# Rebuilding the opening of a cross-attention and mixture-of-experts kernel: load order, weight split and first projections

## The reference

```
x = x + xattn(layernorm(x), ctx)        # 32 batches, 128 tokens, width 128, 16 heads of 64
    # q = xn @ Wq, k = ctx @ Wk, v = ctx @ Wv (W_qkv is 128 x 3072); softmax(q k / 8) v; @ W_out + b_out
x = x + moe(layernorm(x))               # 16 experts, the best 2 of each token, softmax of their two logits
    # gate/up = t @ Wgu[e] + bgu[e]; (clip(up) + 1) * gate * sigmoid(1.702 gate); @ Wd[e] + bd[e]
```

## Time and profile before

| | us |
|---|---|
| median of three runs | 624.29 (623.92 to 624.73) |
| profiled execution, its own time | 624.85 |
| its span, first to last instruction | 623.1 |
| TensorE busy (share of span) | 536.6 (86%) |
| VectorE busy | 535.1 (86%) |
| ScalarE busy | 490.9 (79%) |
| GpSimd busy | 446.2 (72%) |
| DMA at the opening (4 to 12 us) | 300 to 374 GB/s |

### The profile page before, as it was taken

How to read it: one execution, slowest core, us unless ns; L and a number is a source line. 1 busy time by engine, 2 the same in 40 slices (tenths; PEclk the granted TensorE clock), 3 DMA queues, 4 the chain that set the end, 5 groups by cost and what they waited for, 6 DMA issues and landing times.

```text
span 623.1 us, 20538 instructions
## 1 busy us (share of the span) xinstructions
PE 536.6 (86%) x6805; PEld 454.5 (73%) x6806; DVE 535.1 (86%) x1526; ACT 490.9 (79%) x1423; POOL 446.2 (72%) x555
## 2 busy tenths in 40 slices
PE   0689999999999999999999999999756989898700
PEld 0357989888898998988889989998642766666500
DVE  5789999999999999999999999999965877677515
ACT  0479999999999999999999999999832666666500
POOL 7174766689898898988989889877264377777720
PEclk9989999999999999999999999999976999999955
DMA  9689131228316285622932741576012343332149
GB/s 259 188 306 326 28 71 28 43 62 306 84 33 191 60 307 163 228 55 55 312 82 36 251 142 38 145 254 130 3 33 52 91 111 95 94 86 81 41 130 274
DMA packets 76820, 82.14 MB, mean 132 GB/s; under 512 B 8324, under 2 KB 56476, under 8 KB 76724
## 3 DMA queue, kind: packets, MB, share of 16 engines
q1 hardware_dynamic: 63124, 68.13, 38.3%
q0 software_dynamic: 4608, 8.47, 4.2%
q10 hardware_dynamic: 8992, 4.30, 2.6%
HBM read 19.35 MB, written 46.84 MB: 106 GB/s over the span
## 4 chain that ended last, share of the span: by engine, by line
PE 72%; DVE 8%; issue 5%; DMA 5%; ACT 4%; POOL 2%; SPq 2%; ACTq 1%; POOLq 0%; DVEq 0%
PE bank L1156 17%; PE bank L1157 16%; PE bank L1158 16%; PE bank L1252 8%; PE bank L1302 5%; PE bank L1327 3%; PE bank L1335 2%; DMA ctx_sb<-results 2%; DMA ctx_sb<-in_ctx_dram 2%; PE bank L1384 2%; PE bank L1362 1%; PE bank L1166 1%; PE bank L1282 1%; ACT probs L525 1%; POOL places L698 1%
## 5 line engine op out<-in xcount | busy, mean ns | idle before, releaser
L525 ACT ACTIVATE probs<-bank,nbias 128x128 f32<-128x128 f32 x512 | 146.4, 369 | 4.2
L755 POOL DMA_INDIRECT results<-z,stage x80 | 80.3, 1004 | 41.4 <-ACT z L570 23.5
L1000 DVE TENSOR_TENSOR pT<-bank,pT 128x512 f16<-128x512 f32 x128 | 87.2, 682 | 6.5 <-ACT pT L537 5.2
L979 DVE TENSOR_REDUCE qmax<-bank 128x4 f32<-128x512 f32 x128 | 87.0, 679 | 0.0
L1156 PE MATMUL bank<-keys,q_pad 128*128 128x128 f16 x480 | 86.6, 219 | 0.0
L1158 PE MATMUL bank<-keys,q_pad 128*128 128x128 f16 x480 | 86.6, 219 | 0.0
L1157 PE MATMUL bank<-keys,q_pad 128*128 128x128 f16 x480 | 86.6, 219 | 0.0
L537 ACT ACTIVATE pT<-bank 128x512 f16<-128x512 f32 x128 | 78.3, 612 | 4.1 <-PE bank L1252 4.0
L1252 PE MATMUL bank<-ident,probs 128*128 128x128 f32 x512 | 79.2, 278 | 2.2 <-DVE pT L1000 2.1
L698 POOL DMA_INDIRECT places<-payload,slots x64 | 65.4, 1022 | 16.4 <-issue 12.2
L1156 PE MATMUL bank<-xT,w_qkv 128*128 128x256 f16 x256 | 71.7, 280 | 2.6 <-DVE xT L819 1.7
(11 more groups left out here) (220 smaller groups left out, 2007.3 us busy)
## 6 DMA issues: line engine op xcount, KB each, us to landing
places<-z SPq DMA_DIRECT2D x8, 4160.0 KB, 14.7
q_pad<-q_nat SPq DMA_DIRECT2D x120, 128.0 KB, 2.4
stage<-places SPq DMA_DIRECT2D x80, 65.0 KB, 1.9
ctx_sb<-results SPq DMA_DIRECT2D x16, 256.0 KB, 5.7
ctx_sb<-in_ctx_dram ACTq DMA_DIRECT2D x4, 512.0 KB, 10.4
stage<-in_L_ffn_Wgu_dram SPq DMA_DIRECT2D x1, 2048.0 KB, 8.8
out_dram<-x_sb ACTq DMA_DIRECT2D x8, 256.0 KB, 5.4
stage<-in_L_xattn_W_qkv_dram SPq DMA_DIRECT2D x3, 512.0 KB, 6.3
```

What stands on the lines that cost most here:

```text
L525: last = nc.scalar.activation(probs[:, b, k, :], score_bank[b][:, k * P:(k + 1) * P], ACT.Exp, bias=nbias[:, b, k:k + 1], scale=exp_scale)
L755: nc.gpsimd.indirect_dma_start(out=results, out_offset=bass.IndirectOffsetOnAxis(ap=to, axis=0), in_=z[:, (u - 5) % NZ, t, :], in_offset=None,
L979: nc.vector.tensor_reduce(qmax[:, r % 2, :], score_bank[r % 2][:, :].rearrange("p (h k) -> p h k", h=4), AX.X, ALU.max).then_inc(s["qmax_o ...
L1000: nc.vector.tensor_tensor(pT[:, r % 2, LO, :], pt_bank[:, :], pT[:, r % 2, HI, :], ALU.subtract).then_inc(s["pt_lo"], 1)
```

## The change

- SP loads x's four batches ahead of the W thirds. ScalarE's queue issues the five small arrays ahead of ctx. ScalarE runs a tiny activation before its first wait.
- The factor of W is made by itself (`first_spread`, `first_scale`), as soon as the three W thirds are in, with the magnitude of ctx part 0 between its two halves. The factor of ctx follows after part 3.
- ScalarE writes `hi` of thirds 0 and 1 and also scales them in place in fp32; GpSimd scales third 2 in place, and ScalarE then writes its `hi`. GpSimd writes all three `lo` as a plain difference. DVE does none of this.
- GpSimd normalises the rows of pairs 0 and 1 (DVE did).
- ScalarE scales ctx for pair 0 after the W thirds, not before.
- The factors `fac` are made ahead of the first items, from PSUM.
- Four banks, not two, take the first q and k items, so item t waits for the low half of item t - 4. Scores of pair 0 wait for all eight items.
- TensorE runs 13 matmuls of 512 zero columns (`warm`) between and before the first products.

```diff
-        first_bank = (qk_bank, pt_bank)
+        first_bank = (qk_bank, pt_bank, score_bank[0], score_bank[1])
@@ SyncE
+            sp.dma_start(x_sb[:, 0:4, :], x[0:4]...).then_inc(in_x[0], 16)
             for c in range(3): ... W_qkv thirds
-            sp.dma_start(x_sb[:, 0:4, :], x[0:4]...).then_inc(in_x[0], 16)
@@ ScalarE
-            for c in range(4): ... ctx
             ... bout_bc, bg_bc, wg_nat, bgu_sb, bd_sb
+            for c in range(4): ... ctx
+            act.wait_ge(s["zeroed"], 6)
+            nc.scalar.activation(spare[:, :], zeros[:, 0:1], ACT.Copy)
             act.wait_ge(s["scales"], 1)
-            scale_ctx(0)
-            for c in range(3):
+            for c in range(2):
                 nc.scalar.activation(w_qkv[:, HI, third], stage[:, third], ACT.Copy, scale=scale_to[:, 0:1]) -> w_hi
-                if c == 0:
-                    ... xT high half; scale_ctx(1)
+                act.wait_ge(s["w_hi"], c + 1)
+                nc.scalar.activation(stage[:, third], stage[:, third], ACT.Copy, scale=scale_to[:, 0:1]) -> w_scaled
+            act.wait_ge(s["v_scaled"], 1)
+            nc.scalar.activation(w_qkv[:, HI, 2 * INNER:3 * INNER], stage[:, 2 * INNER:3 * INNER], ACT.Copy) -> w_hi
+            act.wait_ge(s["scales"], 2)
+            scale_ctx(0)
+            ... xT high half; scale_ctx(1)
@@ GpSimd
             inverse_root("stat_agg", 2, mv, var_eps, rstd, "rstd_ok", 1)
+            normal_rows(0)
+            pool.wait_ge(s["scales"], 1)
+            nc.gpsimd.tensor_scalar(stage[v third], stage[v third], scale_to[:, 0:1], None, ALU.mult) -> v_scaled
+            for c in range(3):
+                pool.wait_ge(s["w_hi"], c + 1)
+                if c < 2:
+                    pool.wait_ge(s["w_scaled"], c + 1)
+                nc.gpsimd.tensor_tensor(w_qkv[:, LO, third], stage[:, third], w_qkv[:, HI, third], ALU.subtract) -> w_lo
             inverse_root("stat_agg", 4, mv, var_eps, rstd, "rstd_ok", 2)
+            normal_rows(1)
@@ VectorE
+            dve.wait_ge(in_x[0], 16)
+            prep_stats(0)
             for c in range(3): ... W magnitudes
-            ... statistics, ctx magnitudes, both factors, prep_rows(0)
+            magnitude(0, part_largest[:, 0:3])
+            largest_row(score_bank[0])
+            ctx_magnitude(0)
+            first_scale(score_bank[0], 0)
+            for c in range(1, 4):
+                ctx_magnitude(c)
+            magnitude(1, part_largest[:, 3:7])
+            largest_row(score_bank[1])
+            first_scale(score_bank[1], 1)
+            make_factors(score_bank[1])
+            prep_stats(1)
-            qkv_low(0) ... qkv_low(1) ... qkv_low(2), prep_stats(1), prep_rows(1), fac between the items
+            prep_low(0, 0)
+            for t in range(4):
+                first_low(t)
@@ TensorE
-            spread(score_bank[0], 0, 2)
+            def warm(n):
+                for k in range(n):
+                    nc.tensor.matmul(o_bank[:, :], ident16[:, :], zeros[:, :].bitcast(F16)[:, 0:512], start=True, stop=True)
+            def first_spread(bank, k):
+                pe.wait_ge(s["absmax"], k + 1)
+                nc.tensor.transpose(bank[0:1, 0:P], largest[:, k:k + 1], ident[:, :]) -> largest_mm
+                pe.wait_ge(s["row_max_ok"], spreads[0])
+                nc.tensor.matmul(bank[:, P:P + 1], ones2[0:1, :], row_max[0:1, 0:1], start=True, stop=True) -> spread_mm
+            first_spread(score_bank[0], 0)
             pe.wait_ge(s["in_small"], 16 * 5)
             ... transpose of Wg
+            pe.wait_ge(in_ctx[2], 16)
+            warm(7)
+            first_spread(score_bank[1], 1)
+            warm(3)
             prep(0)
+            warm(3)
             for t in range(8):
-                project_qk(0, 0, t, first_bank[t % 2])
+                project_qk(0, 0, t, first_bank[t % 4])
-                    wait(pe, "first_split", t - 1)
+                    wait(pe, "first_split", t - 3)
-                                wait(pe, "first_split", 4 + 2 * r)
+                                wait(pe, "first_split", 8)
```

More of the change, by code:

```diff
@@ L439, in _ @@
             act.dma_start(bd_sb[:, :], bd.rearrange("e (k f) -> (e k) f", k=8)).then_inc(s["in_small"], 16)
+            for c in range(4):
+                act.dma_start(ctx_sb[:, 8 * c:8 * c + 8, :], ctx[8 * c:8 * c + 8].rearrange("b t d -> t b d")).then_inc(in_ctx[c], 16)
+            act.wait_ge(s["zeroed"], 6)
+            nc.scalar.activation(spare[:, :], zeros[:, 0:1], ACT.Copy)
             def scale_ctx(q):
@@ L495, in weights_high @@
                 if (p, r) == (0, 2):
-                    act.wait_ge(s["scales"], 2)
+                    act.wait_ge(s["scales"], 3)
                     nc.scalar.activation(w_out[:, HI].rearrange("p b n -> p (b n)"), stage[:, 3 * INNER:4096], ACT.Copy,
@@ L825, in v_low, with largest_row, first_scale, ctx_magnitude @@
                                         v[:, par, HI, k // 2, heads, 0:DH], ALU.subtract).then_inc(s["misc_free"], 1)
+            def largest_row(bank):
+                spreads[0] += 1
+                dve.wait_ge(s["largest_mm"], spreads[0])
+                nc.vector.tensor_reduce(row_max[0:1, :], bank[0:1, 0:P], AX.X, ALU.max).then_inc(s["row_max_ok"], 1)
+            def first_scale(bank, k):
+                dve.wait_ge(s["spread_mm"], spreads[0])
+                at_top = bank[:, P + 1:P + 2]
+                link(nc.vector.tensor_scalar(at_top, bank[:, P:P + 1], TINY, 1.0 / TOP, ALU.max, ALU.mult))
+                link(nc.vector.tensor_copy(scale_from[:, k:k + 1], at_top))
+                nc.vector.reciprocal(scale_to[:, k:k + 1], at_top).then_inc(s["scales"], 1)
+            def ctx_magnitude(c):
+                dve.wait_ge(in_ctx[c], 16)
+                part_magnitude(ctx_sb[:, 8 * c:8 * c + 8, :].rearrange("p b d -> p (b d)"))
+            def make_factors(bank):
+                both, three_of = bank[:, P + 2:P + 3], bank[:, P + 3:P + 4]
+                link(nc.vector.tensor_tensor(both, bank[:, P + 1:P + 2], scale_from[:, 0:1], ALU.mult))
+                link(nc.vector.tensor_copy(fac[:, 1:2], both))
+                link(nc.vector.tensor_tensor(three_of, both, scale_from[:, 0:1], ALU.mult))
+                link(nc.vector.tensor_copy(fac[:, 4:5], three_of))
+                link(nc.vector.tensor_scalar(fac[:, 0:1], three_of, DH ** -0.5, None, ALU.mult))
+                nc.vector.tensor_scalar(fac[:, 2:3], three_of, -DH ** -0.5, None, ALU.mult).then_inc(s["factors"], 1)
+            dve.wait_ge(in_x[0], 16)
+            prep_stats(0)
             for c in range(3):
@@ L829, in _ @@
                 part_magnitude(stage[:, c * INNER:(c + 1) * INNER])
[L830 to L834, removed]
+            dve.wait_ge(s["part_max"], 3)
+            magnitude(0, part_largest[:, 0:3])
+            dve.wait_ge(s["consts"], 7)
+            largest_row(score_bank[0])
+            ctx_magnitude(0)
@@ L913, in weight_scales @@
                     make_scales(2, 3, "scales")
-                    dve.wait_ge(s["scales"], 2)
+                    dve.wait_ge(s["scales"], 3)
                     link(nc.vector.tensor_tensor(fac[:, 3:4], fac[:, 1:2], scale_from[:, 2:3], ALU.mult))
```

54 lines of the change are left out of this document (17 added, 37 removed).

## The result

After the change the kernel takes 629.08 us (median of 6 runs, 627.61 to 629.89); the kernel before takes 624.76 beside it (6 runs, 623.92 to 626.0). The ratio is 1.0071 (95%: 1.0055 to 1.0087): slower by 4.3 us, where 4.5 off was forecast. The profiled execution took 629.89, the slowest of the six, with a span of 628.0.

The account below looks back on a forecast made before the run. TensorE and DVE were taken as busy throughout the steady part, so the opening adds to the time in full. 4.8 us gained there less 0.3 set aside gave 4.5 off: 619.8 us, range 618.2 to 622.8.

Parts of the forecast that it names:

- After it: After the items: x's other batches land about 31.2, needed at 33.5; clock fall at 42 stays; 0.3 us set aside.
- rival 2: Pair 0: x's rest lands near 35, sharing DMA with Wd and first clear; DVE waits about 1.5; 621.4 us; chance 0.09.
- Its last sentence: Sign of a wrong prediction: shift at 33 us not found at 80, a wait in pair 0 replacing the old one.
- Loads: Opening DMA: last W third lands at 9.3 us (9.1 before), last ctx part at 15.6, 0 to 0.8 late.
- Factor of W: Opening: W's scale factor, made by itself, is out at 13.4 us, 5.9 us earlier.
- ScalarE and GpSimd on W: Opening: GpSimd scales the v third in 3.5 us, differences take 2.2; low halves ready at 19.7, 21.9 and 24.1.
- rival 4: Opening: GpSimd becomes the bound if its four large ops cost about twice as much; slower, 629.8 us; chance 0.09.
- Rivals 1: First items: TensorE's clock rises only near 28.5 us; gain 2.3, time 622.0; chance 0.12.
- The items: Pair 0's projections: first item at 22.5 us, clock up between 21.6 and 25, 13 DVE ops of 0.62 taking 8.1.
- yardstick: End of DVE's last v item in the opening: 32.7 us, 4.8 ahead of 37.48.

Follow-up runs that it names:

- with ctx first: Kernel after with ctx issued ahead of the five small arrays again: 625.65 us, ratio 1.0023 to the kernel before.
- late clear: Kernel after with the second clear issued behind pair 2's q moves: 620.57 us, ratio 0.9936; the same in the kernel before: 624.62 us, 1.0004.
- two ablations: Kernel after with the late clear, without the 13 warm matmuls: ratio 0.9979; with two banks in place of four for the first items: 0.9974.
- all repairs at once: Kernel after with the late clear, small arrays behind ctx, and the transpose of wg_nat behind the first items: 620.67 us, ratio 0.9950.
- versions with ctx's factor 2 us earlier: Late clear, small arrays behind ctx, wg_nat's transpose late: ratio 0.9950; also x behind W: 0.9921; also six warm matmuls behind the second spread: 0.9922.

## Why the prediction was wrong

*The step that failed* is the one headed "After it". It followed x's other batches and the fall of the clock at 42 us and stopped there. It should have gone on along SP's queue. The prediction had x's other batches land 0.6 later (31.2 against 30.6) and saw, in rival 2, that Wd and the first clear would be issued earlier; it asked of them only whether they delay x. The second clear waits for the first to land, on DMA engines that are full from 24 us on in the kernel before (share 1.06), so an earlier issue does not bring it forward: with ctx first, where x's rest is issued as in the kernel before, it is 0.2 later than before. The prediction had the pair steps 4.8 earlier. It let the two run against each other without a look at where they meet. They meet at pair 1's moves, where before has 0.6 us of slack.

An estimate of the wait is the lead of the scores, plus the delay of the clear, less the slack of 0.6. It gives 2.2 + 3.0 - 0.6 = 4.6 for the kernel after (5.4 measured) and 3.7 + 0.2 - 0.6 = 3.3 with ctx first (2.9 measured). By the prediction's own lead of 4.8 it gives 4.4 to 4.8. So the forecast gain could not have passed there, however good the opening. Its last sentence named this symptom, a wait in pair 0 that takes the place of the old one, but gave it no price. The late clear shows that this is the decisive step: without the wait the kernel is 4.05 us faster, and the same move gives the old kernel nothing. That 4.05 lies so near the forecast 4.5 is luck: at the first scores the lead was 3.1, not 4.8. What the wait cost: 5.4 us, and 1.1 more by 71 us, where TensorE's clock was at 1.2 GHz after standing; some of it is caught up by the tables (4.7 to 4.2).

*Loads* were mis-sized, as a term. Forecast: last W third 9.3, last ctx part 15.6 "0 to 0.8 late for the small packets". Measured: 11.38 and 18.29. By the runs that put them back, x ahead of W costs W about 1.2 to 1.45, the small arrays cost ctx 2.55 to 3.0. The five issues took 3.8 us, not 2.3, so ctx's first issue comes at 4.61 instead of 0.79. The mistake was to let ctx land almost on time all the same. In 2 to 6 us few bytes flow in the kernel after, and they are not caught up: the windows 2 to 4 and 4 to 6 us show 77 and 136 GB/s, before it was 257 and 354. That is 0.8 MB less, an estimated 2.1 us at the 380 GB/s around 7 us.

```profile
4.61 8.54 ACTq L439 DMA_DIRECT2D ctx_sb<-in_ctx_dram  x4
```

```profile
2.00:4.00 2.00, 0.00 (x0) 0.00 (x0) 0.00 (x0) 0.00 (x0) 1.86 (x10) 1.00 0.52 77
```

DVE had ctx's maximum at 19.7, not 17.3. From there on the serial path was as forecast: 19.7 to 24.97 is 5.3, against 17.3 to 22.5, 5.2.

*Factor of W*: out at 15.3 against 13.4, late by the load and nothing else (11.38 to 15.3 is 3.9; 9.3 to 13.4 is 4.1).

*ScalarE and GpSimd on W*: right. The v third took 2.85 (3.5 taken, bounds 0.22 and 4.9) and stayed under the 4.1 from which it costs; the differences took 2.1 each (2.2), the last ended at 24.5 (24.1), and no item waited for it. By the Trainium skill's line-rate (GPSIMD Engine Reference, § 4.1 Engine selection) the v third is an estimated 0.9 us, worked out from the same page of the Trainium skill (1.03 cycles an element in § 3.1, 1.2 GHz in § 1 Specifications), and not the prediction's 1.1; the measured 2.85 is three times that, and the measurement decides. The warning of contention in the same page of the Trainium skill (§ 8 Key points), which stood in rival 4, was hardly put to the test: each difference took 2.1, but beside them DVE ran reductions of one input and tiny operations. GpSimd never became the bound; the slower side came true by another mechanism, which no rival named. Rivals 1 and 2 did not come either: the clock was up at 25.8, and x's other batches landed at 33.6, 2.5 us before DVE took them at 36.1.

*The items*: right, as a length. From the first projection to the end of the last v item, 24.97 to 35.12 is 10.15 us; the forecast was 22.5 to 32.7, 10.2; before took 14.6. The clock was up at 25.8, DVE started an op every 0.60 to 0.65. The two ablations give part of it to the warm matmuls (0.8 to 1.3) and the banks (1.4 to 2.0). What the work taken off DVE gave was not measured alone.

*The sum at the last v item*, the prediction's yardstick: 4.8 forecast, 2.4 measured (37.48 to 35.12); the missing 2.4 are the loads, by which DVE had ctx's maximum 2.4 late. With the first projection only 0.55 earlier, the kernel with the late clear led by 3.1 at the first maximum of scores, the kernel after by 2.2.

*What stays open*: why the clock fell between 40 and 45 us in before and after and not in the profiled execution of the late clear (1.8 us in its ledger, which is that of the fastest of five). From the first maximum of scores to the first table, the late clear took 430.9 us and the run without warm matmuls 430.6, both without the fall; with it the run with two banks took 432.2 and all repairs at once 431.4. And why versions with ctx's factor 2 us earlier don't end earlier. In two of them the matmuls of the items were 0.21 apart up to 26.6 and 27.1, and in one of these the factor waited for ScalarE; in the third the first projection ran at full clock and a fall came at 36 to 44 (0.77 and 0.81). That clock and ScalarE eat the gain is argued from these traces, not shown.

## What to carry to other kernels

When a stage is made to end earlier, follow every queue that does not move with it to the next point where it meets the stage: a large transfer that isn't urgent, and starts at a time set by something else, will land on small urgent ones. Price the slack at that point before the gain; here it was 0.6 us and the cure was to move one call, worth 8 us beside the rest of the change. Another queue at the same time was worth half of that. And small transfers at the head of a load queue are not free: issue first what the serial path waits for longest.

## What the runs showed of the hardware

- Five small arrays (104 KB together) issued first delayed 2 MB of ctx on the same queue by 3.0 us in one kernel and 2.55 in the other.
- A 128 KB move landed in 2.4 us in the median, in 8.7 behind a 4.16 MB transfer in its own queue, and in 8.9 beside one from another queue. Behind it, the move landed 1.5 to 2.2 us after the large transfer; beside it, 2.5 us before. The issue took longer too: the first four took 7.1 us in the kernel after, 5.4 in the kernel before and 3.6 with no clear in flight.
- After standing from about 60.5 to 65.9 us, TensorE worked at the 1.2 GHz level until near 70.
- One chip runs the unchanged kernel in 660.69 us, where two others take 624.29 and 624.62. Late clear with small arrays last has a span of 653.4 there, late clear alone 617.2 on the first chip: 36.2 more, of which 5.0 lie ahead of the first placement table (470.50 against 465.50) and 31.2 behind it, in the experts' stretch. The rows of the indirect stores there, of the slow chip and of the first:

```profile
L776 POOL DMA_INDIRECT results<-z,stage x80 | 80.5, 1006 | 71.8 <-ACT z L579 53.5 <-issue 18.3
```

```profile
L776 POOL DMA_INDIRECT results<-z,stage x80 | 80.3, 1004 | 40.9 <-ACT z L579 21.9 <-issue 18.9
```

A store takes the same time; the wait for ScalarE is 31.6 us longer. What makes it late there stays open.
